# Attention 0: a key is made by one VectorE operation, max(min(exponential, 1), k + 1), in place of two

## The reference, cut to what matters

```
q = x @ wq + bq;  k = x @ wk + bk;  v = x @ wv + bv      (x after the layer norm)
Q = elu(q) + 1;   K = elu(k) + 1
KV = sum_s K * v;  Ksum = sum_s K
Z = 1 / (Q * Ksum + 1e-6)
out = gelu((Q * KV * Z) @ wo + bo)
```

## Time and profile before

| what | value |
|---|---|
| median of 3 runs | 1027.86 us (1027.59 to 1030.08) |
| the profiled execution | 1027.37 us |
| its span in the profile | 1025.6 us |
| mean granted PE clock | 0.96 of full |
| attention 0 in it | to about 251 us |

### The profile page before, as it was taken

The page is one execution under the profiler, slowest core; times in us unless marked ns, Lnnn a source line. Parts: engine busy times, 40 slices in busy tenths (PEclk is TensorE's granted clock), DMA queues, the critical chain, the costliest instruction groups (busy, mean ns, idle before and its releaser), DMA issues. The chain is left out here.

```text
span 1025.6 us, 18232 instructions
## 1 busy us (share of the span) xinstructions
PE 889.5 (87%) x6457; PEld 581.0 (57%) x6457; DVE 765.8 (75%) x1505; ACT 528.0 (51%) x782; POOL 459.9 (45%) x607
## 2 busy tenths in 40 slices
PE   5899999997567778469999999998889999999997
PEld 3667677773356655334444444443366667767765
DVE  6788888887389998397888888988667566656642
ACT  3477777775425445427776776766722232223220
POOL 4122222225256666524475566446543553455344
PEclk9899999999689989869999999999989999999999
DMA  9100000000000000762634444310000000000000
GB/s 293 40 11 12 10 10 3 7 11 0 4 0 2 11 1 11 156 151 61 136 86 98 96 108 93 80 35 5 12 10 1 22 21 20 0 20 20 10 11 10
DMA packets 35638, 43.34 MB, mean 42 GB/s; under 512 B 4825, under 2 KB 27769, under 8 KB 35569
## 3 DMA queue, kind: packets, MB, share of 16 engines
q1 hardware_dynamic: 35569, 42.43, 17.0%
HBM read 21.21 MB, written 15.07 MB: 35 GB/s over the span
## 5 line engine op out<-in xcount | busy, mean ns | idle before, releaser
L1633 ACT ACTIVATE PT<-PS 128x1024 f32<-128x1024 f32 x160 | 162.9, 1022 | 67.7 <-PE PS L1417 67.6
L1687 POOL TENSOR_SCALAR_AFFINE_SELECT PT<-PT 128x256 f32<-128x256 f32 (+1 forms) x224 | 97.2, 449 | 131.7 <-ACT PT L1633 130.2
L2088 POOL TENSOR_TENSOR PRE_sb<-PRE_sb,VA 128x512 f32<-128x512 f32 x64 | 82.3, 1288 | 140.2 <-DVE PRE_sb L2154 140.0
L2051 ACT ACTIVATE sg_d<-PS 128x512 f32<-128x512 f32 x64 | 38.3, 598 | 176.5 <-PE PS L1155 176.5
L369 ACT ACTIVATE E<-PS,m 128x512 f32<-128x512 f32 x128 | 87.0, 686 | 41.6 <-PE PS L291 31.6
L2154 DVE TENSOR_TENSOR PRE_sb<-sg_d,PS 128x512 f32<-128x512 f32 x64 | 43.4, 687 | 79.4 <-ACT sg_d L2051 78.1
L496 DVE TENSOR_SCALAR E<-E 128x512 f32<-128x512 f32 x128 | 70.3, 549 | 35.0 <-ACT E L369 30.9
L1724 DVE TENSOR_REDUCE negm<-PS 128x2 f32<-128x1024 f32 x64 | 78.0, 1224 | 23.1 <-PE PS L1406 21.7
L1402 PE MATMUL PS<-kS,qS 48*128 48x384 bf16 (+3 forms) x512 | 74.5, 315 | 23.4 <-DVE spread L1847 9.7
L1432 PE MATMUL PS<-PT,VA 128*32 128x512 f32 (+3 forms) x1024 | 89.3, 444 | 1.7 <-POOL PT L1687 1.7
L406 POOL TENSOR_SCALAR Qs<-Qs 128x1024 f32<-128x1024 f32 x32 | 35.2, 1104 | 113.9 <-ACT Qs L357 113.8
(11 more groups left out here) (300 smaller groups left out, 2280.6 us busy)
## 6 DMA issues: line engine op xcount, KB each, us to landing
qk_rows<-parts SPq DMA_DIRECT2D x32, 192.0 KB, 2.8
qS<-qk_rows SPq DMA_DIRECT2D x32, 192.0 KB, 4.3
kS<-qk_rows SPq DMA_DIRECT2D x32, 192.0 KB, 4.6
xs_sb<-XN_sb SPq DMA_DIRECT2D x23, 256.0 KB, 2.3
qk_rows<-parts SPq DMA_DIRECT2D x32, 128.0 KB, 2.8
X_sb<-in_x_dram SPq DMA_DIRECT2D x8, 256.0 KB, 6.9
qk_rows<-parts SPq DMA_DIRECT2D x32, 64.0 KB, 2.4
out_dram<-X_sb SPq DMA_DIRECT2D x8, 256.0 KB, 2.3
```

Source lines behind the costliest of these rows:

```text
L1633: nc.scalar.activation(PT[:, quad % 2, u, :], PS[:, b:b + 2, :].rearrange("p b n -> p (b n)"), ACT.Exp).then_inc(exp_ready, 1)
L1687: nc.gpsimd.affine_select(out=v, in_=v, pattern=[[0, 4 if u == 4 else 2], [1, P]], compare_op=ALU.is_ge, fill=0.0, base=0, channel_multipl ...
L2088: nc.gpsimd.tensor_tensor(acts[:, s, f, :], acts[:, s, f, :], W[:, slot, s, :], ALU.mult).then_inc(weighted, 1)
```

## The change

In the key half of DVE's turn the two operations become one: L496 isn't done for units 0 to 7, and L503 becomes max(min(E, 1), PSUM), issued as soon as the unit's exponential is there, no longer behind the next unit's L496. The wait for `g_ready` moves to the head of the turn, and `elu_ready` counts the queries only. The query half keeps its operations and their order; L496 of unit 8 is now the first one behind the eight keys.

```diff
--- before.py
+++ after.py
@@ -489,20 +489,23 @@
                 nc.vector.tensor_copy(PRE[:, seq(i)], PS[:, 6, :]).then_inc(out_kept, 1)
 
             def turn(i, slot):
-                for u in range(17):
+                wait_if(dve, g_ready, i)
+                for u in range(8):
+                    n, t = divmod(u, 4)
+
+                    dve.wait_ge(e_ready, i * 16 + u + 1)
+                    nc.vector.scalar_tensor_tensor(out=KB[:, t, n * 512:(n + 1) * 512], in0=E[:, u % RING, :], scalar=1.0,
+                                                   in1=PS[:, RING_BANKS[u % RING], :], op0=ALU.min, op1=ALU.max).then_inc(kq_done, 1)
+                for u in range(8, 17):
                     if u < 16:
                         dve.wait_ge(e_ready, i * 16 + u + 1)
                         e = E[:, u % RING, :]
                         nc.vector.tensor_scalar(e, e, -1.0, 0.0, ALU.add, ALU.min).then_inc(elu_ready, 1)
-                    if u == 0:
-
-                        wait_if(dve, g_ready, i)
+                    if u == 8:
                         continue
-                    n, t = divmod(u - 1, 4)
-                    dve.wait_ge(elu_ready, i * 16 + u)
-                    nc.vector.scalar_tensor_tensor(out=KB[:, t, n * 512:(n + 1) * 512] if u <= 8 else Qs[:, slot, u - 9, :],
-                                                   in0=E[:, (u - 1) % RING, :], scalar=1.0, in1=PS[:, RING_BANKS[(u - 1) % RING], :],
-                                                   op0=ALU.add, op1=ALU.max).then_inc(kq_done, 1)
+                    dve.wait_ge(elu_ready, i * 8 + u - 8)
+                    nc.vector.scalar_tensor_tensor(out=Qs[:, slot, u - 9, :], in0=E[:, (u - 1) % RING, :], scalar=1.0,
+                                                   in1=PS[:, RING_BANKS[(u - 1) % RING], :], op0=ALU.add, op1=ALU.max).then_inc(kq_done, 1)
                     if u == 9 and not is_seq(i, LAST):
                         if is_seq(i, 0):
                             dve.wait_ge(x_loaded, 16 * (NB - 1))
```

## The result

| | before | after |
|---|---|---|
| median, runs of the first comparison | 1028.39 us (4) | 1016.78 us (4; 1014.81 to 1021.01) |
| ratio, 95% interval | | 0.9890 [0.9854, 0.9927] |
| the same kernel, second comparison | 1030.19 us (13) | 1014.57 us (4), 0.9858 [0.9835, 0.9881] |
| third comparison | 1028.27 us (11) | 1016.35 us (6), 0.9881 [0.9857, 0.9906] |
| the profiled execution (span) | 1027.37 (1025.6) | 1021.01 (1019.3) |

The forecast was 1013.3 in a range of 1009.5 to 1019, a ratio of 0.9858 to the 1027.86 of before. The change makes the kernel faster by 11.6 us in the first comparison and by 15.6 and 11.9 in the others; the 14 executions of the changed kernel have a median of 1015.4.

The account below looks back on a forecast made before the run. PE, though busy, was taken to be held by waits for DVE's key operation to free PSUM banks. 4.8 + 1.3 + 5 x 1.41 + 1.4 = 14.6 us off 1027.37 gave 1012.8, stated as 1013.3 for the median; range 1009.5 to 1019.

Parts of the forecast that it names:

- What bounds: Key half of a turn: PE waits 2.1 us, in three waits, for DVE's L503 to free its PSUM bank.
- The cost of the operation: L503 with min, max on the same operands takes 0.68 us, as for the add, max pair.
- Steady turns, 1.41: Repeating turns of attention 0: unit 7 starts at 105.90 instead of 107.31, so 1.41 us less a turn, five times.
- Turn 1, 1.3: Turn 1, slow at its start: unit 7 starts at 50.26 instead of 51.55, 1.3 us gained.
- Turn 0, 4.8: Turn 0: without clips held by POOL's L435, queries start at 20.9 instead of 25.25; 4.8 us, bounds 3.5 and 5.
- The last turn, 1.4: Last turn of attention 0: PE reaches output(6), which DVE's L489 waits for, 1.4 us earlier.
- Sum: All turns of attention 0: 4.8 + 1.3 + 5 x 1.41 + 1.4 = 14.6 us gained.
- All behind shifts as it is: Stages after attention 0: they move earlier with no change in the time they take.
- 1: Turn 0 is held by a load and gains nothing; sum 9.8, time 1018.1; chance 0.09.
- 2: Turns give only half, as another wait (ACT's logarithms or staging DMA) takes the rest; 1018.2 us; chance 0.10.
- 3: No change, 1027.9 us: the removed DVE slot only moves into its wait for ACT; chance 0.03.
- 4: Slower: min, max not one element a cycle in DVE's key slots; loses past 1.37 us a slot; 1049; chance 0.02.

Follow-up runs that it names:

- turns1_only: Against the original kernel: the new key half in turns 1 to 7, the old one in turn 0; 1018.88 us, ratio 0.9908.
- again: The changed kernel run once more with no edit; 1014.57 us, ratio 0.9858 to the original kernel.
- again2: The changed kernel run a third time with no edit; 1016.35 us, ratio 0.9881 to the original kernel.
- turn0_only: Against the original kernel: the new key half in turn 0 alone, the old one in turns 1 to 7; 1024.89 us, ratio 0.9953.
- key_twice: Against the changed kernel: each key's min, max operation done a second time, into a spare tile; one run, 1025.07 us.

## Why the prediction was right, and where a size was off

- **What bounds.** Right. PE's waits for the bank freed by the key operation were the turn's loss, in spite of a busy share of 26.79 of 27.88. With the keys at one operation all of them went but the one at unit 6, which came as walked.
- **The cost of the operation.** Right: 0.687 us for min, max against 0.681.
- **Steady turns, 1.41.** 1.52 measured. The product takes 0.81 us when unit 7 doesn't restart behind a wait; I had taken 0.92 from a product that had just been waited for.
- **Turn 1, 1.3.** 0.79, 0.75 and 0.50 in the three profiles. The walk began at unit 3 at full clock; the half clock lasted over 12 or 13 matmuls instead of 9, and with the keys no longer held by VectorE each of them counts. turns1_only, with 8 of them, shows that the walk's mechanism holds (1.60).
- **Turn 0, 4.8.** Mechanism right, size too high: 3.0 us by the first copy of x in after (41.83 to 38.86), 3.9 in again and in again2, 4.4 in turn0_only. The walk took three things as fixed that aren't, and in after all three cost: the first matmul started 0.57 later by its loads (12.03 against 11.46), 12 slow matmuls ran ahead instead of 10 (0.4), and the staging DMA took 0.98 longer to land. The landing is the largest, and the term that was mis-sized. Where start and landing were as in before (key_twice), the copy came 4.73 earlier. The held L496 of 2.11 us and the queue behind it were as told, and so was the freedom of L503 from POOL. That a figure near 4.8 came out at all has some luck in it: it counts the half clock that the profile of before had from 23 to 26 us as a loss which the change ends, and turns1_only, with the same idle ahead, didn't have it. Against that turn 0 (first copy at 40.92) the new one gains 2.1 us in after, 3.0 in again and again2 and 3.8 in key_twice.
- **The last turn, 1.4.** 12.79 at the stage's end less 11.35 at the last copy is 1.44.
- **Sum.** 14.6 forecast; 12.8, 13.8 and 13.5 at the end of attention 0 in the three profiles. "All behind shifts as it is" held for the work, not for the clock: of these the executions lost 6.4, 1.1 and 1.7 us, net, behind it. The median gave 11.6 us in the first comparison against the 14.6.
- **Rivals.** 1 did not come: the statistics of turn 1 started at 26.11 without a wait for x. 2 did not: the turn gave more than forecast. 3 fell with PE's waits. 4 was far off in fact, but its point is about 1.2 us of slot, not 1.37.

## What to carry to other kernels

Where a producer goes round a small ring of banks, ask how long a bank is held, not how busy the consumer is: here two delays in series (a second operation, and the wait for the next unit's data ahead of it) each hid the gain of removing the other, and VectorE, at 86% of the turn, was not full. A TensorE that shows 96% busy can still give 5%; starts and the waits' releasers tell it. When such a wait goes, look at once for the next tail; here one reordered instruction was worth another 0.5 us a turn.

## What the runs showed of the hardware that I had not expected

- The same kernel loses 1 to 6 us in single executions, against the profile of before, with stretches of 4 to 6 us at a granted clock of 0.51 to 0.78, at places that differ between executions and that had the full clock in others.
- A 256 KB staging DMA landed in 2.4 us or in 3.0 to 3.4; in all eight profiles with 3.0 or more one packet of an instruction queue (0.01 MB) fell in its time, in none of the six with 2.4. That the packet is the cause wasn't tested.
- After an idle of 2.2 us TensorE's granted clock fell to 0.50 for 3 us in one profile (before) and not in another of the same code (turns1_only, idle of 2.26).
- A VectorE operation that reads what the one ahead of it wrote started 0.45 us after it, with an unrelated one between them 0.35 after the nearer.
